# Flamingo block with a routed expert layer: expert rows stored less their own mean, and a join with two VectorE operations a tile

## The reference

```python
def _ln(x, g, b):
    m = x.mean(-1, keepdims=True)
    v = ((x - m) ** 2).mean(-1, keepdims=True)
    return (x - m) / jnp.sqrt(v + EPS) * g + b

def _moe(x, gW, gb, W1, b1, W2, b2):
    ...
    top2_scores, top2_idx = jax.lax.top_k(gates, 2)
    w = (jax.nn.one_hot(top2_idx, NUM_EXPERTS, dtype=xf.dtype) * top2_scores[..., None]).sum(1)
    h = jax.nn.relu(jnp.einsum('nd,edf->enf', xf, W1) + b1[:, None, :])
    y = jnp.einsum('enf,efd->end', h, W2) + b2[:, None, :]
    out = jnp.einsum('ne,end->nd', w, y)
...
x = _ln(src + attn_out, ln1_g, ln1_b)
ff = _moe(x, gW, gb, W1, b1, W2, b2)
return _ln(x + ff, ln2_g, ln2_b)
...
x = x + jnp.tanh(g_ffn[0]) * _L0_ffn_ref(_layernorm(x, axis=-1), ...)
```

## Time and profile before

| | |
|---|---|
| time, median of 3 runs | 1204.14 us (1202.54 to 1205.6) |
| span of the profiled execution | 1214.7 us (the profile gives no other time for this execution) |
| PE busy in the span | 1126.1 us (93%) |
| DVE busy | 827.8 us (68%) |
| ACT busy | 688.4 us (57%) |
| POOL busy | 265.8 us (22%) |
| HBM traffic | 51.32 MB read, 25.90 MB written |

### The profile page before, as it was taken

One profiled execution on the slowest core, in us unless ns is written; L12 is line 12 of the kernel. 1 busy time (PEld: TensorE's weight loads), 2 busy tenths in 40 slices (PEclk: granted clock), 3 DMA queues, 4 the chain that ended last, 5 costly groups with the idle time before them and its releaser, 6 DMA issues.

```text
span 1214.7 us, 36448 instructions
## 1 busy us (share of the span) xinstructions
PE 1126.1 (93%) x12924; PEld 840.5 (69%) x12925; DVE 827.8 (68%) x2431; ACT 688.4 (57%) x1186; POOL 265.8 (22%) x371
## 2 busy tenths in 40 slices
PE   6999999999999999999999999999728999999964
PEld 4576766676766666676666677667517999999942
DVE  5565777776777777667777776777744666666667
ACT  4666767677666667777667776776513333333200
POOL 1011111122212111222212221222321222222233
PEclk9999999999999999999999999999968999999988
DMA  6012043222111111111111011101056222222165
GB/s 149 22 42 68 17 123 105 69 68 74 40 33 37 51 34 33 38 41 34 33 53 38 10 45 46 30 28 64 28 116 187 71 69 71 72 72 71 52 212 159
DMA packets 66597, 79.18 MB, mean 65 GB/s; under 512 B 14008, under 2 KB 52536, under 8 KB 66328
## 3 DMA queue, kind: packets, MB, share of 16 engines
q1 hardware_dynamic: 52680, 54.24, 16.2%
q0 software_dynamic: 6096, 15.66, 3.9%
q10 hardware_dynamic: 7680, 7.34, 1.9%
HBM read 51.32 MB, written 25.90 MB: 64 GB/s over the span
## 4 chain that ended last, share of the span: by engine, by line
PE 75%; issue 9%; DVE 8%; ACT 4%; POOL 1%; DMA 1%; DVEq 0%; another core or an unknown queue 0%; SPq 0%; POOLq 0%; ACTq 0%
PE quad L1299 11%; PE bank L1289 10%; PE bank L1485 9%; PE quad L1497 9%; PE quad L1311 8%; PE sums L1322 6%; PE bank L1436 4%; PE bank L1389 4%; ACT probs L777 4%; PE quad L1308 3%; PE bank L1282 3%; PE bank L1457 2%; PE bank L1322 2%; DVE row_max_C L1050 2%; DVE row_max_C L1047 2%
## 5 line engine op out<-in xcount | busy, mean ns | idle before, releaser
L777 ACT ACTIVATE probs<-quad 125x1792 f32<-125x1792 f32 (+1 forms) x128 | 213.0, 1664 | 116.9 <-PE quad L1311 116.7
L855 ACT ACTIVATE scored_half<-quad 112x750 bf16<-112x750 f32 (+1 forms) x160 | 131.4, 821 | 89.5 <-PE quad L1299 89.0
L1037 DVE TENSOR_REDUCE row_max_A<-quad 112x2 f32<-112x750 f32 x128 | 120.1, 938 | 70.0 <-PE quad L1299 66.5
L1485 PE MATMUL bank<-tile_inT,tile_w 128*128 128x128 f32 x1008 | 124.4, 277 | 0.3 <-ACT tile_w L887 0.3
L1039 DVE TENSOR_REDUCE row_max_A<-scored_half 112x2 f32<-112x750 bf16 x128 | 118.6, 927 | 3.2 <-ACT scored_half L855 1.0
L1485 PEld LDWEIGHTS bank<-tile_inT,tile_w 128*128 128x128 f32 x1008 | 119.0, 194 | 0.7 <-ACT tile_w L887 0.7
L1497 PE MATMUL quad<-output_w,hiddenT 128*128 x504 | 119.1, 380 | 0.0
L1299 PE MATMUL quad<-kT_A,qT_A 32*112 32x375 f32 x1024 | 115.2, 519 | 3.5 <-ACT probs L777 1.5
L1216 DVE TENSOR_SCALAR hiddenT<-bank,hidden_b 128x128 f32<-128x128 f32 x252 | 71.0, 344 | 63.0 <-PE bank L1485 62.6
L1289 PE MATMUL bank<-ctxT,wxk 128*128 128x375 f32 x256 | 99.1, 510 | 5.5 <-DMA bxk<-in_bxk_dram 5.5
L739 POOL DMA_INDIRECT kept_dram<-tile_out,take_back x63 | 60.4, 959 | 186.3 <-DVE tile_out L1239 179.7
(11 more groups left out here) (225 smaller groups left out, 1995.0 us busy)
## 6 DMA issues: line engine op xcount, KB each, us to landing
ctxT<-in_ctxT_dram SPq DMA_DIRECT2D x32, 375.0 KB, 3.5
tile_in<-sent_dram SPq DMA_DIRECT2D x63, 129.0 KB
join_in<-kept_dram SPq DMA_DIRECT2D x28, 256.0 KB, 3.4
hidden_w<-in_hidden_w_dram SPq DMA_DIRECT2D x8, 512.0 KB, 5.0
output_w<-in_output_w_dram SPq DMA_DIRECT2D x8, 512.0 KB, 5.7
x_in<-in_x_dram SPq DMA_DIRECT2D x32, 112.0 KB, 2.9
x_res<-in_x_dram SPq DMA_DIRECT2D x32, 112.0 KB, 3.2
kept_dram<-x_shift SPq DMA_DIRECT2D x32, 112.0 KB
```

The costliest lines, as they stand in the source:

```text
L777: act.activation(probs[0:rows, t.buffer("probs", step), :, :], quad[0:rows, :, 0:U * T], ACT.Exp, scale=SCALE).then_inc(taken[kind_of(step ...
L855: act.activation(scored_half[:, t.buffer("half", step), 0:RT // 2 * n].rearrange("t (r s) -> t r s", s=n), quad[0:T, RT // 2:RT, 0:n], ACT ...
L1037: dve.tensor_reduce(row_max["A"][:, i:P // 2:ROWS], quad[0:T, 0:RT // 2, 0:S], AX_X, ALU.max).then_inc(taken[kind], 1)
L1485: mm = pe.matmul(hidden_bank[k][:, f * P:(f + 1) * P], tile_w[:, k, c, f * P:(f + 1) * P], tile_inT[:, k, c, :], start=c == 0, stop=c == D ...
```

## The change

- In the experts phase `tile_out` is now formed in two steps. `scalar_tensor_tensor` writes `tile_raw` and also gives the sum of each row (`accum_out`, `raw_sum`); a new `tensor_scalar` then stores 256 times the row less its sum, that is, 256 times the row less its mean. A wait on `row_summed` stands between the two.
- In the join the sum of two such rows has mean zero, so no mean is taken. ScalarE squares the bank and sums along the row (`Square` with `accum_out`), over 257 columns: column 256 of each bank holds a constant whose square is the epsilon term, written once by four `memset`.
- GpSimd's power reads `square_mean`. VectorE has two operations left: `join_gain` (bank times inverse deviation times gain) and `result` (plus `x1_in`).
- The plan `JOIN` changes: all of it is stage A, but for the store (`S`), which ScalarE's queue issues two tiles later, behind the square of tile n.

```diff
-JOIN = Plan(JT, 8, JR, {"A": 0, "B": 1}, ["A.add", "B.norm"], {})
+JOIN = Plan(JT, 8, JR, {"A": 0, "S": 2}, ["A.add", "S.store"], {})
...
@@ GpSimd, join @@
-                if t.active("B"):
-                    k = t.slot("B", JR)
-                    pool.wait_ge(join_steady, t.item("B", 1, 1))
-                    if t.later("B", JR):
-                        pool.wait_ge(result_steps, t.item("B", 2, 2 - 2 * JR))
-                    pool.tensor_tensor(join_inv[:, k, :], join_moments[:, k, 1:2], minus_half[:, :],
-                                       ALU.pow).then_inc(join_inverted, 1)
+                if t.active("A"):
+                    k = t.slot("A", JR)
+                    pool.wait_ge(join_squared, t.item("A", 1, 1))
+                    if t.later("A", JR):
+                        pool.wait_ge(join_scaled, t.item("A", 1, 1 - JR))
+                    pool.tensor_tensor(join_inv[:, k, :], square_mean[:, k, :], minus_half[:, :], ALU.pow).then_inc(join_inverted, 1)
@@ ScalarE, join @@
-                if t.active("B"):
-                    n, k = t.item("B"), t.slot("B", JR)
-                    act.wait_ge(result_steps, t.item("B", 2, 2))
+                if t.active("A"):
+                    k = t.slot("A", JR)
+                    act.wait_ge(join_added, t.item("A", 1, 1))
+                    if t.later("A", 2):
+                        act.wait_ge(join_squared, t.item("A", 1, -1))
+                    if t.later("A", JR):
+                        act.wait_ge(join_inverted, t.item("A", 1, 1 - JR))
+                    act.activation(join_square[:, t.slot("A"), :], join_bank[k][:, 0:D + 1], ACT.Square, scale=D ** -0.5,
+                                   accum_out=square_mean[:, k, :]).then_inc(join_squared, 1)
+                if t.active("S"):
+                    n, k = t.item("S"), t.slot("S", JR)
+                    act.wait_ge(result_made, t.item("S", 1, 1))
                     act.dma_start(io["out"][bass.ds(n * P, P), :], result[:, k, :]).then_inc(result_stored[k], DMA)
@@ VectorE, experts @@
-                    dve.scalar_tensor_tensor(tile_out[:, k, :], tile_sum[:, k, :], meta[:, 0:1], tile, ALU.mult, ALU.add).then_inc(tile_done, 1)
+                    dve.scalar_tensor_tensor(tile_raw[:, k, :], tile_sum[:, k, :], meta[:, 0:1], tile, ALU.mult, ALU.add,
+                                             accum_out=raw_sum[:, k, :]).then_inc(row_summed, 1)
+                    dve.wait_ge(row_summed, t.item("D", 1, 1))
+                    dve.tensor_scalar(tile_out[:, k, :], tile_raw[:, k, :], float(D), raw_sum[:, k, :], ALU.mult,
+                                      ALU.subtract).then_inc(tile_done, 1)
@@ VectorE, between the phases @@
+            dve.wait_ge(ex_taken["A.x"], NT)
+            for bank in join_bank:
+                dve.memset(bank[:, D:D + 1], D * TOP * (EPS * D) ** 0.5).then_inc(eps_set, 1)
@@ VectorE, join: bn_stats, bn_aggr, the epsilon add and both scalar_tensor_tensor of before are gone @@
+                if t.active("A"):
+                    k = t.slot("A", JR)
+                    dve.wait_ge(join_inverted, t.item("A", 1, 1))
                     if t.later("A", 2):
-                        dve.wait_ge(join_measured, t.item("A", 2, -2))
...
+                        dve.wait_ge(result_made, t.item("A", 1, -1))
+                    dve.scalar_tensor_tensor(join_gain[:, t.slot("A"), :], join_bank[k][:, 0:D], join_inv[:, k, :], ln2_gain[:, :],
+                                             ALU.mult, ALU.mult).then_inc(join_scaled, 1)
+                    dve.wait_ge(join_scaled, t.item("A", 1, 1))
                     if t.later("A", JR):
...
+                        dve.wait_ge(result_stored[k], t.dmas("A", 0, depth=JR))
+                    dve.tensor_tensor(result[:, k, :], join_gain[:, t.slot("A"), :], x1_in[:, bass.ds(t.item("A", D), D)],
+                                      ALU.add).then_inc(result_made, 1)
@@ TensorE, join @@
                     if t.later("A", JR):
-                        pe.wait_ge(result_steps, t.item("A", 2, 1 - 2 * JR))
+                        pe.wait_ge(join_scaled, t.item("A", 1, 1 - JR))
```

More of the change, by code:

```diff
@@ L384, in build @@
         tile_sum = sb("tile_sum", [P, 2, D])
+        tile_raw, raw_sum = sb("tile_raw", [P, 2, D]), sb("raw_sum", [P, 2, 1])
         tile_out = sb("tile_out", [P, 2, D])
@@ L389, in build @@
         x1_in = sb("x1_in", [P, JT * D])
-        join_stats = sb("join_stats", [P, 2, 6])
-        join_moments = sb("join_moments", [P, JR, 2])
+        join_square, square_mean = sb("join_square", [P, 2, D + 1]), sb("square_mean", [P, JR, 1])
         join_inv = sb("join_inv", [P, JR, 1])
-        join_gain = sb("join_gain", [P, D])
+        join_gain = sb("join_gain", [P, 2, D])
         result = sb("result", [P, JR, D])
@@ L426, in build @@
         join_added = sem("join_added")
-        join_measured = sem("join_measured")
-        join_steady = sem("join_steady")
+        join_squared = sem("join_squared")
         join_inverted = sem("join_inverted")
-        result_steps = sem("result_steps")
+        join_scaled = sem("join_scaled")
+        result_made = sem("result_made")
+        row_summed = sem("row_summed")
+        eps_set = sem("eps_set")
         w_loaded = {n: sem("w_loaded_" + n) for n in ("K", "Q", "V", "B", "C")}
@@ L1241, in _ @@
+                    dve.tensor_scalar(tile_out[:, k, :], tile_raw[:, k, :], float(D), raw_sum[:, k, :], ALU.mult,
+                                      ALU.subtract).then_inc(tile_done, 1)
             EXPERTS.run(dve, expert_turn)
+            dve.wait_ge(ex_taken["A.x"], NT)
+            for bank in join_bank:
+                dve.memset(bank[:, D:D + 1], D * TOP * (EPS * D) ** 0.5).then_inc(eps_set, 1)
             dve.wait_ge(x1_loaded, X1_PARTS * DMA)
             def join_turn(t):
-                a, b = t.active("A"), t.active("B")
@@ L1247, in join_turn @@
-                kA, kB = t.slot("A", JR), t.slot("B", JR)
-                if a:
-                    dve.wait_ge(join_added, t.item("A", 1, 1))
+                if t.active("A"):
+                    k = t.slot("A", JR)
+                    dve.wait_ge(join_inverted, t.item("A", 1, 1))
                     if t.later("A", 2):
-                        dve.wait_ge(join_measured, t.item("A", 2, -2))
-                    dve.bn_stats(join_stats[:, t.slot("A"), :], join_bank[kA][:, 0:D]).then_inc(join_measured, 1)
@@ L1253, in join_turn @@
[L1253 to L1259, removed]
-                    if t.later("A", JR):
[L1261 to L1272, removed]
+                        dve.wait_ge(result_made, t.item("A", 1, -1))
@@ L1512, in join_turn @@
                     mm.then_inc(join_added, 1)
+            pe.wait_ge(eps_set, JR)
             JOIN.run(pe, join_turn)
```

## The result

The changed kernel takes 1198.54 us (median of 4 runs, 1197.64 to 1200.53), beside 1204.15 for the kernel before (4 runs): a ratio of 0.9954, 95% interval 0.994 to 0.9968. Run once more beside other kernels it gave 1198.9 against 1203.4, 0.9959 (0.9947 to 0.9972), 4.5 us under. The change is faster by 5.6 us in the first comparison, as forecast, and by 4.5 in the second.

What follows compares the result with a forecast made beforehand. TensorE was taken to bound the experts phase and VectorE the join. Terms +2.2 + 1.1 - 5.6 - 3.3 = -5.6 us, from 1204.1, gave 1198.5 us, range 1193.5 to 1204.5.

Steps and rivals of the forecast that it cites:

- the queue ring: Experts phase: VectorE's turn, counting its queue's table read, grows from 3.25 to 3.77 us against TensorE's 3.73.
- Term 1: Experts loop: VectorE falls behind TensorE by 0.04 us a turn over 54 looped turns, +2.2 us.
- The gap of 0.52: Experts phase: time from the start of tile_out's first operation to the new tensor_scalar, 0.52 us, added to VectorE's turn.
- the first leg: Experts phase, VectorE's turn: from the start of tile_out to hiddenT, 1.01 us.
- the middle leg: Experts phase, VectorE's turn: from hiddenT to is_spill, taken as 1.30 us, between 1.13 and 1.48.
- Term 2: End of the experts phase: VectorE alone sets the end, so the last tile_out ends later, +1.1 us.
- The accumulator read: Experts phase: the row sum's 0.08 us read, taken to add nothing; rival that it follows the operation: 1202.8 us, chance 0.13.
- The rule that spoke against it: Experts phase, first operation: a row sum with two non-bf16 SBUF sources halves throughput, costing 0.33 us more a turn.
- that rival: Experts phase: the row sum halves the first operation's pace, VectorE's turn 4.10 us, total 1217 us; chance 0.11.
- Term 3: Join, first add to last: 36.1 us in place of 41.70, at 1.32 us a tile, -5.6 us.
- The loads' ring: Join: four load buffers, reused after each add, are the slowest limit, 1.18 to 1.38 us a tile, taken as 1.32.
- Term 4: Join, behind the last add's start: 3.4 us left in place of VectorE's backlog of 6.74, -3.3 us.

Runs made afterwards that it cites:

- e1: The changed kernel with the experts' tile_out formed in one operation as before, new join kept: 1195.07 us, ratio 0.9922 to the kernel before.
- e3: The changed kernel with the tensor_scalar reading the ready tile_sum and no wait between the two operations: 1195.12 us, ratio 0.9928 to the kernel before.
- e4: The changed kernel with the wait and tensor_scalar moved behind the table read for the next tile: 1196.62 us, ratio 0.9936 to the kernel before.
- e7: The changed kernel without the row sum in the first operation, wait and tensor_scalar kept: 1199.27 us, ratio 0.9955 to the kernel before.
- e10: The changed kernel with one more VectorE wait, for the tensor_scalar to end, ahead of the table read: 1219.86 us, ratio 1.0137 to the kernel before.
- e11: The changed kernel timed once more, nothing altered: 1198.9 us, ratio 0.9959 to the kernel before.
- e5: The changed kernel with eight buffers for join_in in place of four: 1196.59 us, ratio 0.993 to the kernel before.
- e9: The changed kernel with the tensor_scalar behind the table read and eight buffers each for join_in and result: 1190.08 us, ratio 0.9883 to the kernel before.

## Why the prediction was right

**VectorE paces the join of before, and the queue ring the experts.** Both held. e1, with the new join and the old experts step, is 9.1 us under before; Terms 3 and 4 made 8.9.

**Term 1, the lag in the loop (+2.2).** Right, and the mechanism was shown, not only the size: the looped turn grew by 0.044 us (0.04 forecast), over 54 turns 2.4 us. The gap of 0.52 was 0.53, the first leg 1.01 was 0.99, the middle leg 1.30 was 1.26. Taking the wait away (e3) or filling it with the read (e4) brings 3.734 back, dropping the sum (e7) does not, and a longer wait (e10) comes out in full.

**Term 2, the end of the phase (+1.1).** Right: 6.72 in place of 5.66 us, 1.1. Together the two terms are 3.5 in this profile; in that of e11 the phase takes 238.6 us, 4.2 over before, with the same 3.78 in the loop, and what is more lies in the turns ahead of the loop.

**The accumulator read** lies within the end of the first operation (it starts 0.41 us behind that operation's start and takes 0.08, and without it the gap shrinks by 0.01 only, e7), the value I had taken. **The new `tensor_scalar`** took 0.35, not the 0.42 of `y`; hidden, so without effect on the ring.

**The rule that spoke against it.** `tile_raw` takes 0.485 us with the row sum, as `tile_out` did without. In e7, which has `tile_raw` without the sum, it takes 0.485 as well. So the row sum does not slow the operation, and that rival falls. The halved pace that the Trainium skill, Vector Engine (DVE) Microarchitecture Reference, section "Points that are easy to get wrong", gives for two SBUF sources that are not bf16 does not show as a price of the sum here.

**Term 3 (-5.6).** 36.26 us from first to last add, 36.1 forecast; 1.33 us a tile, 1.32 forecast. The loads' ring was named rightly: the adds start behind their landings, and e5 sped them up at once. That the size fits to 0.2 us is partly luck. The seven profiles with the new join and this ring of loads (the changed kernel, e1, e3, e4, e7, e10, e11) give 35.5 to 37.5 us, and e11, the same kernel, is at 37.52. One reason for 1.32 was wrong, that at a DMA share of 1.00 and 324 GB/s a tile's bytes need 1.21 us. The changed kernel itself has 4 us with 364 GB/s, and e9 has 8 us with 393, at a share of 1.07. That share did not mark a ceiling; four buffers in flight did. It cost nothing here, since the ring came out slower anyway.

**Term 4 (-3.3).** 3.73 in place of 6.74, so -3.0; the sum of 3.4 was 0.3 short. In the other six of these profiles it is 3.43 to 3.83.

**The rest.** Terms and measures by the profiles: +3.5 - 5.4 - 3.0 = -4.9, and behind the last result 4.24 us in place of 4.67, -0.4, which no term had. That makes -5.3 beside the -5.6 of the medians. The total was met to 0.1 us because such differences cancelled; the second comparison has -4.5. The 10.6 us between the profiled span and the median were carried over as a constant, and this was sound, since they arose in the attention phase. What stays open is why the profiled execution of before was 13 us longer in its attention phase.

## What to carry to other kernels

Count an in-order engine's turn as a ring of starts, not as busy time: here VectorE was 63% busy before the change, and a wait of 0.53 us was already 0.04 a turn more than it could take, because a register load stood behind it in the queue. Put such a load ahead of the wait, so that one covers the other. When a bound falls, list the rings of buffers behind it with the landing time of their transfers: four buffers held the join at 1.33 us a tile, and eight for loads and for stores brought it to 0.99. Then the four banks held it. A busy engine is not yet the bound: look at what each of its operations starts behind.

## What the runs showed that I had not expected

A mean DMA share of 1.00 over 2 us stood with 324 GB/s; shares over 1 with more GB/s stand in e9 above, with twice the buffers, and in this window of the changed kernel:

```profile
1160.00:1164.00 4.00, 3.45 (x14) 2.28 (x15) 2.78 (x7) 1.24 (x6) 2.14 (x3) 1.00 1.04 364
```

The median landing time of a 256 KB load grew from 3.4 us to 3.7 in the changed kernel, 4.7 in e5 and 5.1 in e9:

```profile
DMA to landing us min/median/max: 3.2/5.1/6.7
```

The loads are of one size, so what their landing time gained with more of them in flight is most likely time in which they wait for each other. And a share near 1 did not tell that no more can be moved. Where the ceiling lies, no run here shows: at 393 GB/s the adds of e9 still waited for banks and not for loads.
